# Attention with its softmax sums taken in the first pass over the scores, on one Trainium2 core

## The chip, the core and the metric

The program runs on one core of a Trainium2 chip. Its time is the device time of one execution in microseconds (us), lower is better. The core has five engines that run in parallel, each an in-order queue: TensorE (PE in the profile, with PEld its weight loads), VectorE (DVE), ScalarE (ACT), GpSimd (POOL) and SyncE (SP), which here only issues DMAs. They are kept in step by semaphores. PSUM has eight banks of 128 partitions x 512 fp32 numbers; matmuls write there, ScalarE and VectorE read and write it, GpSimd doesn't.

## What is computed

One block of a diffusion transformer on a batch of 16 sequences of 256 tokens, 512 channels, 16 heads of 32: self-attention, cross-attention to a context of 256 tokens, and a feed-forward layer, each after a modulated layer norm. Cut to what matters:

```python
def _attn(q, k, v):
    scores = jnp.einsum('bqhd,bkhd->bhqk', q, k) / math.sqrt(HEAD_DIM)
    w = jax.nn.softmax(scores, axis=-1)
    return jnp.einsum('bhqk,bkhd->bqhd', w, v).reshape(B, L, D_MODEL)

xn = _adaln(x, noise_emb, ln1_w, ln1_b)          # (x - mu) / std * (1 + gamma) + beta
q, k, v = split(xn @ qkv_w.T)                    # q, k rotated (_rope)
x = x + _attn(_rope(q), _rope(k), v) @ sa_out_w.T
xn = _adaln(x, noise_emb, ln2_w, ln2_b)
x = x + _attn(_rope(xn @ q_w.T), _rope(context @ k_w.T), context @ v_w.T) @ ca_out_w.T
xn = _adaln(x, noise_emb, ln3_w, ln3_b)
x = x + gelu(xn @ ffn_w1.T + ffn_b1) @ ffn_w2.T + ffn_b2
```

## The kernel before

It has two stages. The attention stage, some 1308 us, works off 32 items (16 sequences in each of two layers), and the FFN stage follows. The change touches the attention stage.

Everything is fp32, and products are made of split operands: a number is kept as a high part (rounded to the fast fp32r format) and a low part (the rest), so a projection is three matmuls, hi x hi, hi x lo and lo x hi (L589, L593).

**The order.** `stage_order` writes out one list of steps by hand, and each engine walks that list and picks its own steps. Time is counted in places: three to a head, 48 to an item of 16 heads, 24 to a group G of eight heads (HG = 8), 12 to a half group or quad of four (OH = 4). Part 0 of head n is its scores, part 1 the weigh matmuls of head n - 8 (LAG = 8). In between stand the projections for the items ahead: q at places 52 to 65 (that is 4 to 17 of the next item), v at 66 to 76, the first half of k at 29, the output projection `o` of the item before at 36 to 44, the second half of k at 45.

**A head.** Scores are made twice. The first time (L603, query on the partitions, two matmuls of 256 columns) VectorE takes the row maxima of both halves in one reduction (L851, `neg_max`). For each four heads `max_split` splits the maxima in a high and a low part (L859, L862), `max_turn` transposes them (L612), and `max_copy` has ScalarE copy the eight rows below the queries' 96 rows of `qT`, once for each of the four heads (L729, 8 x 1024). The second time (L623, key on the partitions, 104 rows deep) the maximum is thus taken off inside the matmul, and ScalarE takes the exponential into `prob` (L737).

**The sum.** GpSimd adds the two halves of `prob` (L908). At each `mix`, one for four heads, TensorE multiplies `prob` by the values (L636: 32 columns of the array for each head, four heads side by side, 16 matmul records) into the one bank of `ps_o`, and then multiplies the halves' sums by a matrix of ones (L643, 8 records), which gives the softmax denominators. Then come `invert` (L744 logarithm, L746 exponential of its negative, both ScalarE), `divide` (L867, VectorE), `o_split` (L753, ScalarE) and `o_low` (L896, GpSimd), two places apart.

**Around it.** The modulated norm of x is turned through PSUM in `turn_x` (TensorE L566) and scaled there by ScalarE with gamma and beta from memory (L692). A rotated projection is two VectorE products with cosine and sine (L822, L826), an addition on GpSimd (L902), `rope_high` on ScalarE (L722), `rope_low` on VectorE (L843), a spill to DRAM and later a stacked load into `qT` and `kT` by SyncE.

**Banks.** Four banks of `ps_s` go round among scores, weigh and max_turn (`score_bank`); TensorE waits until the user four turns back has been read (`scores_left`). Three banks `ps_g` serve the projections, one is `ps_o`.

## Time and profile before

| | before |
|---|---|
| times of three runs | 1989.99, 1990.77, 1994.31 us |
| median | 1990.77 us |
| span of the profiled execution | 1991.3 us |
| TensorE busy | 1955.2 us |
| VectorE busy | 1335.1 us |
| ScalarE busy | 1221.5 us |
| GpSimd busy | 1097.4 us |

The profiled execution took 0.5 us more than the median. In the rows below a group of instructions has the form: line, engine, operation, output <- inputs, shapes, count | busy us in all, mean ns of one | idle time of the engine just before them, and what ended it. Busy time counts overlapping instructions once, so busy time over count can be less than the mean of one.

### The profile page before, as it was taken

The numbers are of one execution on the slowest core, as the hardware profiler recorded it, in microseconds if no ns is written. First come the engines' busy times: TensorE is split into PE (matmuls) and PEld (weight loads), VectorE is DVE, ScalarE is ACT, GpSimd is POOL, SyncE is SP. The second block draws the span as 40 slices with busy tenths as digits, with TensorE's granted clock in tenths as the row PEclk, the third lists the DMA queues.
The fourth block names the chain that finished last, engine by engine and source line by source line (L and its number), as shares of the span: only waits on it lengthen the run. The fifth ranks groups of instructions, "written<-read, shape, count | busy, mean of one in ns | idle before, by whom it ended". The sixth has DMA issues, their size and how long they took to land. (4 is left out here: it accounts for less than half of the span.)

```text
span 1991.3 us, 40759 instructions
## 1 busy us (share of the span) xinstructions
PE 1955.2 (98%) x14612; PEld 1666.6 (84%) x14612; DVE 1335.1 (67%) x2317; ACT 1221.5 (61%) x2277; POOL 1097.4 (55%) x1205
## 2 busy tenths in 40 slices
PE   7999999999999999999999999899999999999999
PEld 6788888888887888888888887678998989989998
DVE  6866776776677676666667666545676676666654
ACT  3565566666666666666666666655656666666654
POOL 2555566566666676766666676523444363553531
PEclk9999999999999999999999999999999999999999
DMA  7877667676778686667667676543322323232230
GB/s 245 219 203 182 173 172 193 162 192 177 179 196 224 174 222 192 180 192 207 186 173 206 190 180 177 152 133 97 115 82 78 107 64 96 85 95 88 63 96 32
DMA packets 300197, 307.53 MB, mean 154 GB/s; under 512 B 15840, under 2 KB 253664, under 8 KB 300000
## 3 DMA queue, kind: packets, MB, share of 16 engines
q1 hardware_dynamic: 299408, 304.45, 55.4%
q8 instruction: 121, 1.98, 0.4%
q14 instruction: 76, 0.62, 0.1%
q10 hardware_dynamic: 592, 0.47, 0.1%
HBM read 212.59 MB, written 92.27 MB: 153 GB/s over the span
## 5 line engine op out<-in xcount | busy, mean ns | idle before, releaser
L908 POOL TENSOR_TENSOR sums_sb<-prob 128x256 f32<-128x256 f32 x512 | 405.1, 796 | 323.1 <-ACT prob L737 321.8
L851 DVE TENSOR_REDUCE neg_max<-ps_s 128x2 f32<-128x512 f32 x512 | 347.7, 686 | 335.2 <-PE ps_s L603 332.8
L737 ACT ACTIVATE prob<-ps_s 128x512 f32<-128x512 f32 x512 | 304.6, 596 | 348.6 <-PE ps_s L623 343.3
L902 POOL TENSOR_TENSOR rope_c<-rope_c,rope_s 128x512 f32<-128x512 f32 x128 | 179.0, 1398 | 115.9 <-DVE rope_s L826 115.1
L603 PE MATMUL ps_s<-kT,qT 96*128 96x256 f32 x1024 | 225.0, 301 | 2.3 <-DMA qT<-q_turned 2.3
L603 PEld LDWEIGHTS ps_s<-kT,qT 96*128 96x128 f32 x1024 | 164.5, 190 | 65.5 <-issue 53.9
L623 PE MATMUL ps_s<-qT,kT 104*128 104x256 f32 x1024 | 207.7, 284 | 10.0 <-ACT qT L729 7.2
L593 PE MATMUL ps_g<-xx_hi,w_hi 128*128 128x256 f32 x1024 | 210.4, 287 | 3.4 <-DVE rope_s L826 2.0
L593 PE MATMUL ps_g<-xx_hi,w_lo 128*128 128x256 f32 x1024 | 205.4, 282 | 0.0
L593 PE MATMUL ps_g<-xx_lo,w_hi 128*128 128x256 f32 x1024 | 204.8, 281 | 0.0
L1266 PE MATMUL ps_y<-w_hi,h_hi 128*128 128x512 f32 x512 | 201.5, 393 | 1.2 <-DVE h_lo L1391 1.2
L623 PEld LDWEIGHTS ps_s<-qT,kT 104*128 104x128 f32 x1024 | 170.6, 190 | 36.4 <-ACT qT L729 13.9
L1266 PE MATMUL ps_y<-w_lo,h_hi 128*128 128x512 f32 x512 | 200.6, 392 | 0.0
L1266 PE MATMUL ps_y<-w_hi,h_lo 128*128 128x512 f32 x512 | 199.4, 389 | 0.0
L1391 DVE TENSOR_TENSOR h_lo<-h_sb,h_hi 128x512 fp32r<-128x512 f32 x128 | 111.2, 872 | 103.7 <-ACT h_hi L1289 102.4
L1250 PE MATMUL ps_h<-xf_hi,cw_hi 128*128 128x256 f32 x592 | 167.4, 283 | 0.0
L1250 PE MATMUL ps_h<-xf_lo,cw_hi 128*128 128x256 f32 x592 | 165.8, 280 | 0.0
L1250 PE MATMUL ps_h<-xf_hi,cw_lo 128*128 128x256 f32 x592 | 165.7, 280 | 0.0
L593 PEld LDWEIGHTS ps_g<-xx_hi,w_hi 128*128 128x128 f32 x1024 | 158.4, 190 | 8.5 <-issue 5.2
L593 PEld LDWEIGHTS ps_g<-xx_lo,w_hi 128*128 128x128 f32 x1024 | 158.7, 191 | 0.0
L593 PEld LDWEIGHTS ps_g<-xx_hi,w_lo 128*128 128x128 f32 x1024 | 158.0, 190 | 0.0
L729 ACT ACTIVATE qT<-ps_s 8x1024 fp32r<-8x1024 f32 x128 | 130.4, 1018 | 3.1
(157 smaller groups left out, 4823.7 us busy)
## 6 DMA issues: line engine op xcount, KB each, us to landing
kT<-k_turned SPq DMA_DIRECT2D x192, 256.0 KB, 4.8
qT<-q_turned SPq DMA_DIRECT2D x64, 512.0 KB, 7.0
f_raw<-in_w1T SPq DMA_DIRECT2D x124, 256.0 KB, 3.1
k_turned<-rot_hi SPq DMA_DIRECT2D x64, 256.0 KB, 4.2
k_turned<-rot_lo SPq DMA_DIRECT2D x64, 256.0 KB, 4.3
q_turned<-rot_hi SPq DMA_DIRECT2D x64, 256.0 KB, 2.5
q_turned<-rot_lo SPq DMA_DIRECT2D x64, 256.0 KB, 2.6
qT<-q_turned SPq DMA_DIRECT2D x64, 256.0 KB, 7.5
```

What stands on the lines that cost most here:

```text
L593: ins = eng.matmul(ps_g[:, b, s * L:(s + 1) * L], w[:, row, (T * s + t) * P:(T * s + t + 1) * P], a[:, c, :], start=c == 0 and j == 0 and ...
L603: ins = eng.matmul(ps_s[:, score_bank(step), t * L:(t + 1) * L], qT[0:ROWS, G % NG, j, t * P:(t + 1) * P], kT[0:ROWS, G % NG, j, :], start ...
L623: ins = eng.matmul(ps_s[:, score_bank(step), t * L:(t + 1) * L], kT[:, G % NG, j, t * P:(t + 1) * P], qT[:, G % NG, j, :], start=True, sto ...
L729: eng.activation(qT[ROWS:MROWS, G % NG, OH * half:OH * (half + 1), :], ps_s[ROWS:MROWS, score_bank(step), 0:L].unsqueeze(1).broadcast_to([ ...
L737: eng.activation(prob[:, n % NP, :, :].rearrange("p t l -> p (t l)"), ps_s[:, score_bank(step), :], ACT.Exp, scale=HD ** -0.5).then_inc(ex ...
L851: eng.tensor_reduce(neg_max[G % 2][:, :, j], ps_s[:, score_bank(step), :].rearrange("p (t l) -> p t l", l=L), AX.X, ALU.max, negate=True). ...
L902: eng.tensor_tensor(rope_c[n % 2][:, :, :], rope_c[n % 2][:, :, :], rope_s[:, :, :], ALU.add).then_inc(rope_added, 1)
L908: eng.tensor_tensor(sums_sb[:, n % NP, :], prob[:, n % NP, 0, :], prob[:, n % NP, 1, :], ALU.add).then_inc(halves_added, 1)
L1250: ins = eng.matmul(ps_h[:, bank(p, n), 0:L], w[:, cols], x_[:, k, :], start=n in OPENS and k == 0 and j == 0, stop=k == 1 and j == 2, skip ...
L1266: ins = eng.matmul(ps_y[:, t, :], h[:, t * P:(t + 1) * P], w, start=c == 0 and j == 0, stop=c == FC - 1 and j == 2)
L1391: eng.tensor_tensor(h_lo[a % NH][:, :], h_sb[a % 2][:, :], h_hi[a % NH][:, :].bitcast(F32), ALU.subtract).then_inc(h_lo_done, 1)
```

## The change

The softmax denominators come from the first pass. A new step `total` has ScalarE run over each score bank in place after the maximum: exponential with the negative maximum as bias and an accumulated sum, one instruction for each half (256 columns). For four heads a step `log` takes the logarithm of the sums, and `max_split` takes it off the negative maxima before it splits them. So the second pass gives normalised weights at once: the addition on GpSimd, the ones matmuls, `invert` and `divide` are gone. The scale of the scores moves into cosine and sine on the host.

`mix` now takes eight heads, 32 matmul records, into a bank of `ps_s`, which has five banks and one more kind of user; `prob` holds ten heads. `o_split` and `o_low` work on 512 columns straight from PSUM, `o_low` on VectorE. `max_copy` writes one head's rows (256 columns), and `max_spread` has VectorE copy them to the other three. `turn_x` is scaled by VectorE from item 2 on. `rope_low` moves from VectorE to GpSimd, whose rotary addition becomes a subtraction and an addition of half the width. Some projections stand one place later. Not shown: the narrower sine, buffers that hold the first parameters, the names of semaphores, and the same shifts by one place on other lines.

```diff
+BY_ACT = 2
...
-            late = {N: 24, N + 1: 14}.get(ahead, 0)
+            late = {N: 26, N + 1: 14}.get(ahead, 0)
...
-                turns(shares((p + 29, 6, k[:4]), (p + 45, 7, k[4:])))
+                turns(shares((p + 29, 6, k[:4]), (p + 46, 7, k[4:])))
...
-            spread(p + 36, 9, [("project", "o", i - 1, t, c) for cs in (range(KC - 1), (KC - 1,)) for t in range(T) for c in cs])
-            put(p + 47, "store", i - 1)
+            spread(p + 37, 9, [("project", "o", i - 1, t, c) for cs in (range(KC - 1), (KC - 1,)) for t in range(T) for c in cs])
+            put(p + 48, "store", i - 1)
...
-            put(24 * G + 12 * half + 10, "max_split", G, half)
+            put(24 * G + 12 * half + 12, "log", G, half)
+            put(24 * G + 12 * half + 13, "max_split", G, half)
             put(24 * G + 12 * half + 19, "max_turn", G, half)
             put(24 * G + 12 * half + 20, "max_copy", G, half)
+            put(24 * G + 12 * half + 23, "max_spread", G, half)
...
-    for quad in range(4 * N):
-        place = 3 * (4 * quad + LAG + 5) + 2
-        for n, kind in enumerate(("mix", "invert", "divide", "o_split", "o_low")):
-            put(place + 2 * n, kind, quad)
+    for G in range(2 * N):
+        place = 3 * (8 * G + LAG + 9) + 2
+        for n, kind in enumerate(("mix", "o_split", "o_low")):
+            put(place + n, kind, G)
...
+            if part == 2 and n < HEADS:
+                yield ("total", n)
...
-    score_users = [step for step in order if step[0] in ("scores", "weigh", "max_turn")]
+    score_users = [step for step in order if step[0] in ("scores", "weigh", "max_turn", "mix")]
     score_turn = {step: n for n, step in enumerate(score_users)}
-    NS = 4
+    NS = 5
...
-            NP = 6
+            NP = 10
...
-                return {"scores": max_done, "weigh": exp_done, "max_turn": maxes_copied}[old[0]], nth[old]
+                return {"scores": total_done, "weigh": exp_done, "max_turn": maxes_copied, "mix": o_lo_done}[old[0]], nth[old]
...
-                        if j % OH == 0:
-                            eng.wait_ge(maxes_copied, nth["max_turn", G, j // OH])
+                        if j % OH < 2:
+                            eng.wait_ge(maxes_spread if j % OH else maxes_copied, nth["max_turn", G, j // OH])
...
-                        quad = step[1]
-                        i, c = divmod(quad, KC)
-                        eng.wait_ge(exp_done, OH * (quad + 1))
-                        if c == 0:
+                        G = step[1]
+                        i, g = divmod(G, 2)
+                        b = score_bank(step)
+                        eng.wait_ge(exp_done, HG * (G + 1))
+                        if g == 0:
                             eng.wait_ge(v_done, values[i, 1])
-                        if quad:
-                            eng.wait_ge(o_divided, quad)
-                        for k in range(T):
-                            for j in range(OH):
-                                ins = eng.matmul(ps_o[j * HD:(j + 1) * HD, 0, 0:L],
-                                                 v_sb[i % NV][:, k, c * P + j * HD:c * P + (j + 1) * HD],
-                                                 prob[:, (OH * quad + j) % NP, k, :], start=k == 0, stop=k == T - 1)
-                        if quad == 0:
-                            eng.wait_ge(ones_set, 1)
-                        eng.wait_ge(halves_added, OH * (quad + 1))
-                        for j in range(OH):
-                            ins = eng.matmul(ps_o[j * HD:(j + 1) * HD, 0, L:2 * L], ones[:, :],
-                                             sums_sb[:, (OH * quad + j) % NP, :], start=True, stop=True)
-                        ins.then_inc(mix_done, 1)
+                        for c in (2 * g, 2 * g + 1):
+                            cols = slice((c % 2) * L, (c % 2 + 1) * L)
+                            for k in range(T):
+                                for j in range(OH):
+                                    n = OH * (KC * i + c) + j
+                                    ins = eng.matmul(ps_s[j * HD:(j + 1) * HD, b, cols],
+                                                     v_sb[i % NV][:, k, c * P + j * HD:c * P + (j + 1) * HD],
+                                                     prob[:, n % NP, k, :], start=k == 0, stop=k == T - 1)
+                            ins.then_inc(mix_done, 1)
...
+                        if i >= BY_ACT:
+                            continue
...
-                        eng.activation(qT[ROWS:MROWS, G % NG, OH * half:OH * (half + 1), :],
-                                       ps_s[ROWS:MROWS, score_bank(step), 0:L].unsqueeze(1).broadcast_to([2 * OH, OH, L]),
+                        eng.activation(qT[ROWS:MROWS, G % NG, OH * half, :], ps_s[ROWS:MROWS, score_bank(step), 0:L],
                                        ACT.Copy).then_inc(maxes_copied, 1)
+                    elif kind == "total":
+                        n = step[1]
+                        G, j = divmod(n, HG)
+                        eng.wait_ge(max_done, n + 1)
+                        if j == 0 and G >= 2:
+                            eng.wait_ge(log_done, 2 * (G - 1))
+                        scores = ps_s[:, score_bank(("scores", n)), :]
+                        for t in range(T):
+                            ins = eng.activation(scores[:, t * L:(t + 1) * L], scores[:, t * L:(t + 1) * L], ACT.Exp,
+                                                 bias=neg_max[G % 2][:, t, j:j + 1], accum_out=total[G % 2][:, t, j:j + 1])
+                        ins.then_inc(total_done, 1)
+                    elif kind == "log":
+                        G, half = step[1:]
+                        eng.wait_ge(total_done, HG * G + OH * (half + 1))
+                        if nth[step] > 2:
+                            eng.wait_ge(shift_done, nth[step] - 2)
+                        eng.activation(log_sb[half][:, :, :], total[G % 2][:, :, OH * half:OH * (half + 1)], ACT.Ln).then_inc(log_done, 1)
                     elif kind == "weigh":
                         n = step[1]
                         eng.wait_ge(weigh_done, n + 1)
                         if n >= NP:
                             eng.wait_ge(mix_done, (n - NP) // OH + 1)
-                        eng.activation(prob[:, n % NP, :, :].rearrange("p t l -> p (t l)"), ps_s[:, score_bank(step), :], ACT.Exp,
-                                       scale=HD ** -0.5).then_inc(exp_done, 1)
-                    elif kind == "invert":
-                        quad = step[1]
-                        eng.wait_ge(mix_done, quad + 1)
-                        if quad:
-                            eng.wait_ge(o_lo_done, quad)
-                        eng.activation(o_sb[:, :], ps_o[:, 0, L:2 * L], ACT.Ln).then_inc(log_done, 1)
-                        eng.wait_ge(log_done, quad + 1)
-                        eng.activation(o_sb[:, :], o_sb[:, :], ACT.Exp, scale=-1.0).then_inc(den_inverted, 1)
+                        eng.activation(prob[:, n % NP, :, :].rearrange("p t l -> p (t l)"), ps_s[:, score_bank(step), :],
+                                       ACT.Exp).then_inc(exp_done, 1)
                     elif kind == "o_split":
-                        quad = step[1]
-                        i, c = divmod(quad, KC)
-                        eng.wait_ge(o_divided, quad + 1)
-                        if i and c == 0:
+                        G = step[1]
+                        i, g = divmod(G, 2)
+                        eng.wait_ge(mix_done, 2 * (G + 1))
+                        if i and g == 0:
                             eng.wait_ge(product_done, products["o", i - 1, 1])
-                        eng.activation(o_hi[:, c, :], o_sb[:, :], ACT.Copy).then_inc(o_hi_done, 1)
...
-                    elif kind == "rope_low":
-                        n = ropes[step[1:]]
-                        if n > NT:
-                            eng.wait_ge(*rot_free(n))
-                        eng.wait_ge(rot_hi_done, n)
-                        eng.tensor_tensor(rot_lo[:, n % NT, :, :], rope_c[n % 2][:, :, :],
-                                          rot_hi[:, n % NT, :, :].bitcast(F32), ALU.subtract).then_inc(rot_lo_done, 1)
...
                         eng.wait_ge(max_done, HG * G + OH * (half + 1))
                         if nth[step] > 1:
                             eng.wait_ge(max_turned, nth[step] - 1)
+                        eng.wait_ge(log_done, nth[step])
                         mine = neg_max[G % 2][:, :, OH * half:OH * (half + 1)]
-                        eng.tensor_reduce(max_parts[:, :, ROWS:ROWS + OH].bitcast(F32R), mine.unsqueeze(3), AX.X,
+                        eng.tensor_tensor(shift[:, :, :], mine, log_sb[half][:, :, :], ALU.subtract).then_inc(shift_done, 1)
+                        eng.wait_ge(shift_done, nth[step])
+                        eng.tensor_reduce(max_parts[:, :, ROWS:ROWS + OH].bitcast(F32R), shift[:, :, :].unsqueeze(3), AX.X,
                                           ALU.max).then_inc(max_hi_done, 1)
                         eng.wait_ge(max_hi_done, nth[step])
-                        eng.tensor_tensor(max_parts[:, :, ROWS + OH:MROWS], mine, max_parts[:, :, ROWS:ROWS + OH],
+                        eng.tensor_tensor(max_parts[:, :, ROWS + OH:MROWS], shift[:, :, :], max_parts[:, :, ROWS:ROWS + OH],
                                           ALU.subtract).then_inc(max_split, 1)
-                    elif kind == "divide":
-                        quad = step[1]
-                        eng.wait_ge(den_inverted, quad + 1)
-                        eng.tensor_tensor(o_sb[:, :], ps_o[:, 0, 0:L], o_sb[:, :], ALU.mult).then_inc(o_divided, 1)
+                    elif kind == "o_low":
+                        G = step[1]
+                        eng.wait_ge(o_hi_done, G + 1)
+                        chunks = slice(2 * (G % 2), 2 * (G % 2) + 2)
+                        eng.tensor_tensor(o_lo[:, chunks, :], ps_s[:, score_bank(("mix", G)), :].rearrange("p (c l) -> p c l", l=L),
+                                          o_hi[:, chunks, :].bitcast(F32), ALU.subtract).then_inc(o_lo_done, 1)
+                    elif kind == "turn_x" and step[1] >= BY_ACT:
+                        i, half = step[1:]
+                        layer, b = divmod(i, B)
+                        if half == 0:
+                            eng.wait_ge(mod_added, nth["mod_add", layer, 1])
+                            if i < B or i >= N_ITEMS:
+                                eng.wait_ge(x_low_done, nth["x_low", i - 1, 1])
+                            else:
+                                eng.wait_ge(ctx_low_done, 2 * (i - B + 1))
+                        eng.wait_ge(x_turned, nth[step])
+                        for c in range(2):
+                            k = 2 * half + c
+                            ins = eng.tensor_scalar(xT[:, k, :], ps_g[:, bank(step), c * L:(c + 1) * L],
+                                                    gb[:, layer, k, b:b + 1], gb[:, layer, KC + k, b:b + 1], ALU.mult, ALU.add)
+                        ins.then_inc(x_full, 1)
+                    elif kind == "max_spread":
+                        G, half = step[1:]
+                        eng.wait_ge(maxes_copied, nth[step])
+                        rows = qT[ROWS:MROWS, G % NG, OH * half:OH * (half + 1), :]
+                        eng.tensor_copy(rows[:, 1:OH, :], rows[:, 0:1, :].broadcast_to([2 * OH, OH - 1, L])).then_inc(maxes_spread, 1)
...
-                    elif kind == "o_low":
-                        quad = step[1]
...
-                        eng.tensor_tensor(rope_c[n % 2][:, :, :], rope_c[n % 2][:, :, :], rope_s[:, :, :], ALU.add).then_inc(rope_added, 1)
-                    elif kind == "weigh":
-                        n = step[1]
-                        eng.wait_ge(exp_done, n + 1)
-                        if n >= NP:
-                            eng.wait_ge(mix_done, (n - NP) // OH + 1)
-                        eng.tensor_tensor(sums_sb[:, n % NP, :], prob[:, n % NP, 0, :], prob[:, n % NP, 1, :],
-                                          ALU.add).then_inc(halves_added, 1)
+                        eng.tensor_tensor(rope_c[n % 2][:, 0, :], rope_c[n % 2][:, 0, :], rope_s[:, 0, :], ALU.subtract)
+                        eng.tensor_tensor(rope_c[n % 2][:, 1, :], rope_c[n % 2][:, 1, :], rope_s[:, 1, :], ALU.add).then_inc(rope_added, 1)
+                    elif kind == "rope_low":
...
```

## Rows read from the trace of the kernel before

**Rows 1.** Busy us of each engine, share of the span, instructions; from the page.

```profile
PE 1955.2 (98%) x14612; PEld 1666.6 (84%) x14612; DVE 1335.1 (67%) x2317; ACT 1221.5 (61%) x2277; POOL 1097.4 (55%) x1205
```

**Rows 2.** Stretches: length; busy us (instructions) of PE, PEld, DVE, ACT, POOL; clock, DMA, GB/s.

```profile
100.00:1250.00 1150.00, 1140.66 (x9409) 952.33 (x9407) 798.13 (x1459) 729.49 (x1344) 741.03 (x824) 1.00 0.71 188
295.39:305.88 10.49, 10.49 (x78) 8.48 (x77) 6.03 (x12) 8.58 (x17) 7.04 (x8) 1.00 0.60 201
305.88:315.98 10.10, 10.10 (x79) 8.27 (x78) 6.63 (x11) 5.45 (x10) 6.88 (x10) 1.00 0.83 178
315.98:325.43 9.45, 9.45 (x85) 8.24 (x84) 7.20 (x17) 4.52 (x8) 4.61 (x7) 1.00 0.53 159
325.43:333.91 8.48, 8.48 (x83) 7.56 (x82) 7.17 (x13) 5.45 (x10) 5.20 (x6) 1.00 0.73 173
```

**Rows 3.** Timeline of TensorE around one mix: start, us, line, operation.

```profile
498.18 0.40 PE L593 MATMUL ps_g<-xx_lo,w_hi 128*128 128x256 f32 x2
498.51 1.07 PE L636 MATMUL ps_o<-prob,v_sb 128*32 128x256 f32 x16
499.40 0.61 PE L643 MATMUL ps_o<-sums_sb,ones 128*32 128x256 f32 x8
499.94 0.50 PE L603 MATMUL ps_s<-kT,qT 96*128 96x256 f32 x2
```

**Rows 4.** Slices of that mix: L636's matmuls alone on TensorE.

```profile
498.58:498.64 0.06, 0.06 (x4) 1.00 0.56 119
498.88:498.94 0.06, 0.06 (x8) 1.00 1.09 375
```

**Rows 5.** Groups of TensorE's instructions, whole span.

```profile
L643 PE MATMUL ps_o<-sums_sb,ones 128*32 128x256 f32 x1024 | 79.3, 381 | 0.9 <-POOL sums_sb L908 0.9
L603 PE MATMUL ps_s<-kT,qT 96*128 96x256 f32 x1024 | 225.0, 301 | 2.3 <-DMA qT<-q_turned 2.3
```

**Rows 6.** Groups of ScalarE's instructions, whole span.

```profile
L737 ACT ACTIVATE prob<-ps_s 128x512 f32<-128x512 f32 x512 | 304.6, 596 | 348.6 <-PE ps_s L623 343.3
L729 ACT ACTIVATE qT<-ps_s 8x1024 fp32r<-8x1024 f32 x128 | 130.4, 1018 | 3.1
L692 ACT ACTIVATE xT<-ps_g,gb 128x256 f32<-128x256 f32 x136 | 69.1, 560 | 24.4 <-PE ps_g L566 23.9 <-DVE gb L797 0.5
L746 ACT ACTIVATE o_sb<-o_sb 128x256 f32<-128x256 f32 x128 | 53.6, 418 | 4.0
L744 ACT ACTIVATE o_sb<-ps_o 128x256 f32<-128x256 f32 x128 | 48.6, 379 | 1.3 <-PE ps_o L643 1.3
L1371 ACT ACTIVATE h_sb<-ps_h,b_sb 128x256 f32<-128x256 f32 x56 | 26.4, 472 | 61.5 <-PE ps_h L1250 61.5
```

**Rows 7.** Timeline of ScalarE, two neighbours that don't depend on each other.

```profile
303.44 0.60 ACT L737 ACTIVATE prob<-ps_s 128x512 f32<-128x512 f32 x1
303.93 0.59 ACT L715 ACTIVATE v_sb<-ps_g 128x512 f32<-128x512 f32 x1
```

**Rows 8.** Groups of VectorE's instructions; L862 by its least, median and longest ns.

```profile
L843 DVE TENSOR_TENSOR rot_lo<-rope_c,rot_hi 128x512 fp32r<-128x512 f32 x128 | 106.2, 830 | 17.4 <-ACT rot_hi L722 17.4
L867 DVE TENSOR_TENSOR o_sb<-ps_o,o_sb 128x256 f32<-128x256 f32 x128 | 53.2, 416 | 8.9 <-ACT o_sb L746 8.8
...
L862 DVE TENSOR_TENSOR max_parts<-neg_max,max_parts x128: 166/482/1182, 56.0 to 1289.4; 128x8 f32<-128x8 f32 x128
```

**Rows 9.** Groups of GpSimd's instructions, whole span.

```profile
L908 POOL TENSOR_TENSOR sums_sb<-prob 128x256 f32<-128x256 f32 x512 | 405.1, 796 | 323.1 <-ACT prob L737 321.8
L902 POOL TENSOR_TENSOR rope_c<-rope_c,rope_s 128x512 f32<-128x512 f32 x128 | 179.0, 1398 | 115.9 <-DVE rope_s L826 115.1 <-issue 0.3
```

**Rows 10.** Waits of TensorE's weight loads: us in all, times, longest.

```profile
PEld ps_s L623 <- ACT qT L729: 13.9, 21, 2.3
```

**Rows 11.** Stretches near the end of the attention stage.

```profile
1218.87:1287.82 68.95, 63.53 (x535) 50.82 (x534) 49.31 (x95) 47.35 (x89) 42.40 (x50) 1.00 0.66 161
1232.93:1239.96 7.03, 6.13 (x63) 5.07 (x62) 6.90 (x12) 4.92 (x10) 6.36 (x8) 1.00 0.33 110
```

67 lines of the change are left out of this document (33 added, 34 removed).

## The prediction

> **What bounds the kernel now.** I read the page's busy shares first: TensorE is busy for 98% of the span, the next engine for 67% [rows 1]. The table of stretches then says how full the other engines are in the attention stage: between 100 and 1250 us TensorE is busy 1140.66 of 1150 us, VectorE 798.13, ScalarE 729.49, GpSimd 741.03, at a granted clock of 1.00 [rows 2]. So TensorE sets the time, and only 9.3 us of that stretch are its idle time. The kernel repeats itself with a period of one batch item, 38.5 us. I cut one item at the four first mix matmuls of its mixes and get quarters of 10.49, 10.10, 9.45 and 8.48 us, with ScalarE busy for 8.58, 5.45, 4.52 and 5.45 of them [rows 2]; counted back from the hand-written order, these are places 17-29, 29-41, 41-53 and 5-17 of an item's 48. The FFN stage behind attention isn't touched. The chain of the page ends in that stage and so says nothing on the change; I don't use it.
>
> **What leaves TensorE.** Ahead of a mix the last two projection matmuls start at 498.18 and, one step of 0.12 later, 498.30; the 16 mix matmuls start at 498.51, the 8 ones matmuls at 499.40, the next scores at 499.94 [rows 3]. A matmul of this shape lasts 0.38 us (the group of the ones matmuls, [rows 5]), and slices of 60 ns show 4 of them running at first and 8 later [rows 4]: four column groups start together, a new round before the last has ended. 16 matmuls in 1.07 us make four rounds: (1.07 - 0.38) / 3 = 0.23, and 0.89 / 4 = 0.222 us a round. The whole place from 498.30 to 499.94 is 1.64 us, of which 0.12 is the normal step, so a mix of four heads costs 1.52 us: 0.21 to the first round, five steps of 0.222, 0.32 from the last round to the next work, less 0.12. The new mix of eight heads has eight rounds and one entry and exit: 0.21 + 7 x 0.222 + 0.32 - 0.12 = 1.96 us, in place of 2 x 1.52 = 3.04. Saved: 1.08 us for each of 64 groups of eight heads, **69 us**. By item, TensorE falls from 38.5 to 36.3 us. The ones matmuls' own group is busy 79.3 us [rows 5], but that counts the last one's full 0.38 us, which overlaps its neighbours. Mix matmuls, scores, weigh and projections keep their counts.
>
> **What ScalarE gets.** Per item it is now busy 729.49 / 1150 x 38.5 = 24.4 us [rows 2]. Leaving: the logarithm 4 x 0.38, its exponential 4 x 0.42, the copy of maxima 4 x 1.02, o_split 4 x 0.42 (a copy of the exponential's size), and turn_x 69.1 / 34 = 2.03 [rows 6]. Coming: copies of 256 columns on 8 partitions, priced as the 128x256 row at 4 x 0.38; o_split in halves, 2 x 0.60; the new logarithm of 8 numbers per partition, between its fixed part, 0.16 (0.379 - 256 x (0.596 - 0.379) / 256 = 0.16), and 0.38, taken as 0.30, 4 times. That leaves 17.35 us an item before the new sums. These are 32 half-score exponentials per item, 128x256, PSUM to PSUM, with a bias from memory and an accumulated sum. The nearest row is GELU from PSUM with a bias, 472 ns against 379 without [rows 6], and ScalarE starts an independent instruction 0.11 us before the last ends (303.44 + 0.60 against 303.93) [rows 7], so 0.38 us in pace. No row shows an accumulated sum. Bounds: 0 and the fixed part of one more instruction, 0.16, with the overlap lost (0.63 in all). I take 0.10 more, 0.48 us: nearer to the plain row, since it is the same engine pass. 32 x 0.48 = 15.4, ScalarE 32.7 of 36.3 us an item, **90%**; at 0.38 it is 29.5 us (81%), at 0.63 it is 37.5 us (103%).
> The Trainium skill, "ScalarE: Activation LUTs", sections "Step-by-step: what each stage is for" and "What ACT_TABLE_LOAD costs", says that each pointer operand adds about 93 ns, that neighbours overlap by as much, and that writing PSUM is quicker than SBUF; the first two agree with [rows 6, 7], and no run here shows the third yet. By its formula a half would take about an estimated 0.40 us in pace, without the sum; the accumulated sum has no price there.
>
> **Where ScalarE binds inside an item.** The quarters don't share evenly, and the mixes now sit at places 5 and 29 only. TensorE: 10.49 - 1.52 = 9.0; 10.10 - 1.52 + 1.96 = 10.5; 9.45 - 1.52 = 7.9; 8.48 - 1.52 + 1.96 = 8.9. ScalarE, quarter by quarter: old time, less 1.86 for logarithm, exponential, o_split and the smaller copy, less 2.03 of turn_x in the first, plus 0.3 for the log, 0.6 for o_split in the second and fourth, plus 8 x 0.48: 8.8, 8.3, 6.8, 8.3. So in the first quarter the two engines are nearly even, in the other three TensorE is clearly the longer. What decouples them: five score banks shared by everything, so that weigh matmul k + 5 turns needs the total of a score made 7 places earlier, and the weigh at place 25 needs the maxima copied at place 20, 5 places or 3.8 us ahead. TensorE waited for that copy before too: 13.9 us, 21 times, up to 2.3, with ScalarE at 63% [rows 10]. With ScalarE at 90% I add half a microsecond an item, **+15 us** over 30 items (bounds: 0, since no quarter is longer on ScalarE, and 1.6 us an item, rival B).
>
> **VectorE and GpSimd.** VectorE loses rot_lo (4 x 0.83 an item) and the division (4 x 0.42), and gets turn_x (4 x 0.42, priced as the division row, one 256-column pass from PSUM), o_low (2 x 0.7, between the division's 0.42 and rot_lo's 0.83 at twice the division's columns), the spread (4 x 0.6, from the same two rows) and the shift [rows 8]. The shift is one more 8-element subtraction; the one that exists takes 166, 482 or 1182 ns (min, median, max) [rows 8], so 4 x 0.5. From 26.7 to 29.2 us an item, 80% of 36.3: hidden behind TensorE, and if that cover went it would cost its 2.5 us. GpSimd loses 16 x 0.79 and gains rot_lo at about 1.3 a piece against 1.40 for its 512-column addition [rows 9], some 15 of 36.3 us: hidden. What is queued behind the new waits: max_split on VectorE now waits for the log on ScalarE; behind it stand the next score maxima and the rotary products, which free the projection banks. SyncE's spills stand 0.5 us longer for rot_lo, and with them the stacks, the x loads and the stores queued behind; TensorE waited 2.3 us in all for stacks before [rows 5], so 0.5 us stays covered.
> The Trainium skill, "SBUF — State Buffer", in its terms (shared port pair), speaks against the shift: a VectorE instruction with two SBUF inputs and a GpSimd one that reads SBUF exclude each other. The 166 to 1182 ns agree, and by that rule each shift may wait out a GpSimd instruction; with the sums gone it would meet fewer.
>
> **Ends.** From 1218.87 to 1287.82 us few projections are left: TensorE is busy 63.53 of 68.95 us, ScalarE 47.35 [rows 11]. For eight quarters ScalarE gets 8 x (3.84 - 1.26) = 20.6 more, less 2.0 of turn_x: 66 us, against 68.95 less 8 x 0.54 = 64.6 for the stretch if TensorE set it. The light quarter of 7.03 us (ScalarE 4.92) [rows 11] goes to 7.5, not to 6.5. Taking the longer engine in each of the eight gives about no gain there: **+4 us** on the sum. The start has a chain of rotations through GpSimd, with 1.3 in place of 0.83 us for rot_lo and some queueing: **+1**. The last mix is followed by two steps, not four, but leaves two chunks of the output projection behind it: 0. Edits with one answer: sine and cosine scaled on the host, the narrower sine, parameter loads all into prob, places moved by one: 0.
>
> **Sum.** The profiled execution spans 1991.3 us, 0.5 above the median of the three, 1990.77. 1991.3 - 69 + 4 + 1 + 15 = 1942.3, less 0.5 = **1942 us** rounded.
>
> **Rivals.**
> A. ScalarE binds: the accumulated sum is an instruction of its own without overlap. For: no row prices it. At 0.63 us a half 37.5 us an item, 1.2 above TensorE, 30 x 1.2 = 36, with 14 for ends (10) and start (4), estimates scaled up from the 4 and 1 above: 1991 - 69 + 14 + 36 = 1972. It begins at (36.3 - 17.35) / 32 = 0.59 us a half. Against: that lies 0.11 us above the price taken, more than a second memory operand costs (0.09).
> B. The new chain (total, log, shift, split, turn, copy, spread) locks the engines: VectorE stands at max_split while ScalarE is behind, ScalarE then lacks the next maximum. Against: ten places, 7.5 us, from scores at 9 to max_turn at 19, hold a 512-column VectorE pass (0.83 at most, [rows 8]), 0.96, 0.3 and three small passes, 2.6 to 4.6 us. If each of four times an item costs 0.4 us, 1.6 x 32 = 51 in place of 15: 1978.
> C. Slower: the exponential that reads and writes one PSUM bank runs at half rate: 0.48 + 256 x 0.85 / 1000 = 0.70 us. ScalarE 17.35 + 22.4 = 39.7 an item against the old 38.5: 32 x 1.2 + 5 + 6: 2040. It decides from (38.5 - 17.35) / 32 = 0.66 us a half. Against: this kernel has no such instruction to judge by, but reading PSUM alone is no slower than SBUF (379 against 418 ns, [rows 6]). The Trainium skill, "PSUM — Partial Sum Buffer", section "Specifications (TRN2)", names full bandwidth unless two engines meet in one bank, and here only one is in the bank.
> D. It doesn't do what it says: the ones rounds were filling time that TensorE would spend waiting anyway. The 100% busy quarters say no [rows 2]; it would be 1991.
>
> **Chances.** Forecast, with 1916 to 1958 of its own: 0.65. A or B, 1958 to 1986: 0.21. D or a half-way mix within 0.2% (1987 to 1995; 0.2% is about what a measurement of this kernel can tell from no change): 0.05. C and other slower outcomes: 0.09. Range 1916 to 1985: its low end is the whole 69 with most of the 9.3 us of TensorE's idle time gone too as the copy gets shorter, its high end A or B with some more of the ends' cost. Faster 0.86, same 0.05, slower 0.09.
>
> **What would show it.** Right: TensorE's attention stage shorter by 50 or so, no ones row, one 32-matmul mix of about 1.9 us; total rows at 0.45 to 0.5 us; ScalarE near 90%; VectorE near 80%. Wrong: total rows above 0.59 us, or TensorE idle for more than 1 us an item at weigh or scores, released by ScalarE; or a period of the steady items that isn't near 36.8 us.

## The result and the profile after

| | before | after |
|---|---|---|
| median | 1991.30 us (4 runs) | 1967.95 us (4 runs, 1963.51 to 1972.09) |
| span of the profiled execution | 1991.3 us | 1961.7 us |

The ratio is 0.9878, with a 95% interval of 0.986 to 0.9896: faster by 1.2%, 23 us, where the prediction said 2.5%, 49 us. The time lies in the range and near none of the rivals but A (1972), whose mechanism turns out to be the wrong one. The profiled execution was the fastest of the four, 4.4 us under their median; sums below are made on the spans: 1991.3 - 1961.7 = 29.6 us gained.

The page of the changed kernel, busy us of each engine, to be held against [rows 1], and two rows of its slices of the span:

```profile
PE 1902.3 (97%) x13588; PEld 1653.0 (84%) x13588; DVE 1418.4 (72%) x2509; ACT 1458.3 (74%) x4005; POOL 783.0 (40%) x820
...
PE   7899999999999999999999998899999999999999
...
PEclk9899999999999999999999999999999999999999
```

TensorE did 1024 fewer matmuls and was busy 52.9 us less, not 69. Its idle time went from 1991.3 - 1955.2 = 36.1 to 59.4 us. Both halves of the shortfall stand there already: 23.3 us more of standing still, and 16.2 us more of busy time than the count of matmuls explains. The attention stage in one row, and the two halves of an item in each layer, cut at its mixes (columns as in [rows 2]):

```profile
100.00:1250.00 1150.00, 1120.23 (x8729) 962.26 (x8729) 906.51 (x1699) 984.14 (x3050) 459.45 (x478) 0.99 0.75 194
346.40:364.28 17.88, 17.88 (x141) 15.36 (x140) 13.27 (x28) 15.15 (x50) 3.43 (x4) 1.00 0.82 217
364.28:383.63 19.35, 18.98 (x149) 16.16 (x149) 15.58 (x29) 16.28 (x50) 10.73 (x11) 1.00 0.64 150
842.08:860.15 18.07, 17.79 (x121) 14.48 (x120) 14.28 (x29) 15.02 (x49) 5.59 (x6) 1.00 0.92 268
860.15:878.78 18.63, 18.63 (x170) 17.30 (x169) 15.53 (x28) 17.24 (x53) 10.88 (x12) 1.00 0.60 136
```

An item lasts 37.2 us in layer 0 and 36.7 in layer 1, where 36.3 was forecast without stalls. ScalarE is busy for 31.4 of 37.2 us (84%) and VectorE for 28.9 (77%). TensorE's idle time in the long stretch is 29.8 us, 9.3 before [rows 2].

The parts of the change, as the trace has them. First TensorE's timeline around a mix (start, us, line, operation), then groups of the whole span on ScalarE, VectorE and GpSimd:

```profile
346.07 0.40 PE L597 MATMUL ps_g<-xx_lo,w_hi 128*128 128x256 f32 x2
346.40 1.93 PE L642 MATMUL ps_s<-prob,v_kept 128*32 128x256 f32 x32
348.27 0.50 PE L607 MATMUL ps_s<-kT,qT 96*128 96x256 f32 x2
```

```profile
L738 ACT ACTIVATE ps_s<-ps_s,neg_max 128x256 f32<-128x256 f32 x1024 | 459.3, 451 | 85.1 <-DVE neg_max L853 81.6
L738 ACT ACTIVATION_READ_ACCUMULATOR ps_s<-ps_s,neg_max 128x1 f32 x1024 | 213.7, 209 | 0.0
L728 ACT ACTIVATE qT<-ps_s 8x256 fp32r<-8x256 f32 x128 | 48.3, 378 | 3.1
L746 ACT ACTIVATE log_sb<-total 128x8 f32<-128x8 f32 x128 | 26.7, 209 | 3.8
...
L894 DVE CAST qT<-qT 8x768 fp32r<-8x768 f32 x128 | 121.4, 949 | 9.8 <-ACT qT L728 6.3
L887 DVE TENSOR_SCALAR xT<-ps_g,gb 128x256 f32<-128x256 f32 x128 | 63.3, 537 | 0.0
L862 DVE TENSOR_TENSOR shift<-neg_max,log_sb 128x8 f32<-128x8 f32 x128 | 48.2, 376 | 38.7 <-ACT log_sb L746 36.8
L873 DVE TENSOR_TENSOR o_lo<-ps_s,o_hi 128x512 fp32r<-128x512 f32 x64 | 43.7, 683 | 12.7 <-ACT o_hi L760 12.7
...
L930 POOL TENSOR_TENSOR rot_lo<-rope_c,rot_hi 128x512 fp32r<-128x512 f32 x128 | 165.8, 1300 | 50.2 <-ACT rot_hi L721 49.1
```

From the last projection pair at 346.07 to the mix are 0.33 us and from there to the scores 1.87; less two normal steps of 0.12 that is 1.96 us, the mix of the sum. Two halves of one total on ScalarE:

```profile
350.26 0.45 ACT L738 ACTIVATE ps_s<-ps_s,neg_max 128x256 f32<-128x256 f32 x1
350.62 0.20 ACT L738 ACTIVATION_READ_ACCUMULATOR ps_s<-ps_s,neg_max 128x1 f32 x1
350.71 0.45 ACT L738 ACTIVATE ps_s<-ps_s,neg_max 128x256 f32<-128x256 f32 x1
```

And who kept TensorE's weight loads waiting (us, times, longest), to be held against [rows 10]:

```profile
PEld ps_s L607 <- ACT ps_s L738: 19.4, 34, 1.8
PEld ps_s L627 <- ACT ps_s L738: 13.1, 17, 1.7
```

The wait for the copied maxima is gone as a large one, and the total, which now keeps a score bank, has taken its place.

**Where the gain went.** The mix of group G stands at the same place as the second mix of its pair did before, so their starts cut both traces at the same points. "Due" is the length before less 1.08 us for each of the groups in it (for the first stretch less one mix of four, 1.52; for the last plus 0.44, the longer mix):

| stretch, by the start of a mix | before | due | after | lost | of it idle |
|---|---|---|---|---|---|
| start to G 0 | 87.20 | 85.68 | 97.26 | 11.6 | 6.6 |
| G 0 to 8 | 161.18 | 152.54 | 155.32 | 2.8 | 0.9 |
| G 8 to 24, layer 0 | 308.20 | 290.92 | 297.86 | 6.9 | 3.1 |
| G 24 to 34, change of layers | 202.74 | 191.94 | 199.77 | 7.8 | 5.3 |
| G 34 to 56, layer 1 | 427.06 | 403.30 | 403.05 | -0.3 | 2.7 |
| G 56 to 63, end | 115.59 | 108.03 | 117.05 | 9.0 | 3.3 |
| G 63 to the end of the program | 689.33 | 689.77 | 691.39 | 1.6 | 1.4 |

That is 39.5 us lost out of 69.1. 28.4 of them lie in three short stretches, at the start, at the change of layers and at the end, which together make a fifth of the program; the long stretch of layer 1 came out at what was due. Idle is not all of it. TensorE's own rows, columns: length, busy (instructions), granted clock, DMA share, GB/s:

```profile
50.00:55.00 5.00, 3.62 (x22) 0.61 1.10 343
55.00:60.00 5.00, 5.00 (x33) 0.71 1.11 218
85.00:90.00 5.00, 3.03 (x11) 0.52 0.83 268
90.00:95.00 5.00, 5.00 (x25) 0.50 0.74 182
615.00:620.00 5.00, 2.13 (x13) 0.77 0.97 238
620.00:625.00 5.00, 5.00 (x18) 0.55 1.11 278
1165.00:1170.00 5.00, 1.95 (x9) 0.73 0.53 115
1170.00:1175.00 5.00, 4.98 (x41) 0.59 0.95 320
```

Between 90 and 95 us TensorE worked without a gap at 1.2 GHz. Taken over all the 5 us stretches, TensorE had some 37 us of time at 1.2 GHz, all in these three parts of the program, against 3 before. These are six episodes of 3.4 to 10.2 us, each beside a stop of TensorE of 1.2 to 3.4 us: behind it, or begun in its last microsecond. Not every such stop has one: behind those of 1.4 to 1.9 us that end at 66, 76, 606, 721 and 1195 us the clock stayed at 1.00 in this execution. The busy time above the due one in the same three parts is 5.0, 2.6 and 5.7 us. (Not all of such an excess is the clock: G 8 to 24 has one of 3.8 us at a clock of 1.00. A matmul's span of 0.40 overlaps the next, 0.24 later, so a stop shorter than the overlap counts as busy.) The traces of the experiments, which follow, go the same way. In the end stretch, G 56 to 63, TensorE does the same 782 matmuls in e10, e9, after and e12; it was busy there for 99.1, 100.4, 103.1 and 104.5 us, at a mean granted clock of 0.99, 0.96, 0.94 and 0.93.

### The profile page after: what moved, and what is told of

Same layout as the page of the kernel before. It is cut to its first block and busy times, and to the rows that moved or that the text cites. A ratio compares the mean times of both kernels' runs of the same rounds, so it can differ in the third digit from the quotient of the medians.

```text
span 1961.7 us, 39861 instructions
## 1 busy us (share of the span) xinstructions
PE 1902.3 (97%) x13588; PEld 1653.0 (84%) x13588; DVE 1418.4 (72%) x2509; ACT 1458.3 (74%) x4005; POOL 783.0 (40%) x820
## 5 line engine op out<-in xcount | busy, mean ns | idle before, releaser
L738 ACT ACTIVATE ps_s<-ps_s,neg_max 128x256 f32<-128x256 f32 x1024 | 459.3, 451 | 85.1 <-DVE neg_max L853 81.6
L853 DVE TENSOR_REDUCE neg_max<-ps_s 128x2 f32<-128x512 f32 x512 | 352.7, 690 | 162.7 <-PE ps_s L607 158.8
L923 POOL TENSOR_TENSOR rope_c<-rope_c,rope_s 128x256 f32<-128x256 f32 x128 | 98.6, 770 | 425.2 <-DVE rope_s L834 425.2
L627 PE MATMUL ps_s<-qT,kT 104*128 104x256 f32 x1024 | 213.8, 291 | 21.0 <-ACT ps_s L738 6.4
L607 PE MATMUL ps_s<-kT,qT 96*128 96x256 f32 x1024 | 218.0, 295 | 10.7 <-DMA qT<-q_turned 5.4
L607 PEld LDWEIGHTS ps_s<-kT,qT 96*128 96x128 f32 x1024 | 172.3, 193 | 54.8 <-ACT ps_s L738 19.4
L738 ACT ACTIVATION_READ_ACCUMULATOR ps_s<-ps_s,neg_max 128x1 f32 x1024 | 213.7, 209 | 0.0
L627 PEld LDWEIGHTS ps_s<-qT,kT 104*128 104x128 f32 x1024 | 168.8, 193 | 50.6 <-issue 19.4
L930 POOL TENSOR_TENSOR rot_lo<-rope_c,rot_hi 128x512 fp32r<-128x512 f32 x128 | 165.8, 1300 | 50.2 <-ACT rot_hi L721 49.1
```

Of the source, the lines that this page charges most:

```text
L607: ins = eng.matmul(ps_s[:, score_bank(step), t * L:(t + 1) * L], qT[0:ROWS, G % NG, j, t * P:(t + 1) * P], kT[0:ROWS, G % NG, j, :], start ...
L627: ins = eng.matmul(ps_s[:, score_bank(step), t * L:(t + 1) * L], kT[:, G % NG, j, t * P:(t + 1) * P], qT[:, G % NG, j, :], start=True, sto ...
L738: ins = eng.activation(scores[:, t * L:(t + 1) * L], scores[:, t * L:(t + 1) * L], ACT.Exp, bias=neg_max[G % 2][:, t, j:j + 1], accum_out= ...
L853: eng.tensor_reduce(neg_max[G % 2][:, :, j], ps_s[:, score_bank(step), :].rearrange("p (t l) -> p t l", l=L), AX.X, ALU.max, negate=True). ...
L923: eng.tensor_tensor(rope_c[n % 2][:, 0, :], rope_c[n % 2][:, 0, :], rope_s[:, 0, :], ALU.subtract)
L930: eng.tensor_tensor(rot_lo[:, n % NT, :, :], rope_c[n % 2][:, :, :], rot_hi[:, n % NT, :, :].bitcast(F32), ALU.subtract).then_inc(rot_lo_d ...
```

## The experiments

Each was timed in three rounds beside the kernel before; times are medians. "After" is the changed kernel, 1968 us. The lengths are those of the stretches of the table above, from each profiled execution; since after's lies 4.4 us under its median, a gain on after looks smaller by about that much in the stretches than in the medians, and a loss larger:

| kernel | us | ratio, 95% interval | to G 0 | 0-8 | 8-24 | 24-34 | 34-56 | 56-63 |
|---|---|---|---|---|---|---|---|---|
| after | 1967.95 | 0.986-0.9896 | 97.3 | 155.3 | 297.9 | 199.8 | 403.1 | 117.1 |
| e1 ones off | 1939.12 | 0.9726-0.9758 | 86.1 | 154.2 | 294.3 | 193.6 | 408.0 | 109.8 |
| e2 first 8 low parts | 1958.98 | 0.9826-0.9855 | 92.1 | 155.3 | 297.7 | 199.8 | 403.6 | 118.0 |
| e3 no read | 1956.07 | 0.9803-0.9833 | 98.3 | 153.7 | 294.5 | 197.2 | 401.2 | 118.4 |
| e4 filling | 1970.01 | 0.9877-0.9906 | 100.2 | 158.6 | 297.7 | 201.3 | 403.1 | 117.1 |
| e5 four banks | 2007.87 | 1.0065-1.0095 | 98.7 | 160.5 | 308.1 | 207.3 | 417.2 | 121.7 |
| e6 x by ScalarE | 1980.22 | 0.9925-0.9955 | 96.8 | 156.9 | 300.9 | 201.1 | 409.8 | 119.5 |
| e7 whole copy | 1986.26 | 0.9957-0.9978 | 97.4 | 157.9 | 305.7 | 202.3 | 409.8 | 120.3 |
| e8 rounds back | 2017.91 | 1.0115-1.0145 | 100.2 | 162.3 | 311.5 | 205.2 | 422.1 | 123.8 |
| e9 no total | 1941.47 | 0.9732-0.9766 | 96.0 | 153.0 | 293.1 | 193.5 | 399.3 | 114.0 |
| e10 total aside | 1954.30 | 0.9796-0.9826 | 97.5 | 153.0 | 293.1 | 200.1 | 403.6 | 114.3 |
| e11 all low parts | 1960.84 | 0.9828-0.9857 | 88.9 | 156.3 | 299.8 | 202.1 | 403.8 | 117.2 |
| e12 total first | 1956.20 | 0.9798-0.9831 | 88.8 | 154.7 | 296.5 | 201.5 | 405.0 | 118.6 |

**Is the work that left worth its time?** e1 takes the ones matmuls and their additions out of the kernel before and changes nothing else. It leaves out the softmax denominators; the logarithm becomes a copy of the same size, so that ScalarE keeps its work.

```diff
-                        for j in range(OH):
-                            ins = eng.matmul(ps_o[j * HD:(j + 1) * HD, 0, L:2 * L], ones[:, :],
-                                             sums_sb[:, (OH * quad + j) % NP, :], start=True, stop=True)
...
-                    elif kind == "weigh":
...
-                        eng.activation(o_sb[:, :], ps_o[:, 0, L:2 * L], ACT.Ln).then_inc(log_done, 1)
+                        eng.activation(o_sb[:, :], ps_o[:, 0, 0:L], ACT.Copy, scale=0.0).then_inc(log_done, 1)
```

> The kernel before without the ones matmuls (8 records at each of 128 mixes) and without GpSimd's additions of the halves; the logarithm is replaced by a copy with scale 0 of the same size, so the values aren't divided. It measures the first term of my sum alone: two rounds of 0.222 us at each mix, 128 x 0.444 = 57 us, with the four-head mixes kept. If the term is right: 1934 us, ratio 0.971. If the ones rounds filled time that TensorE would have lost anyway (rival D): above 1970 us.

It gave 52.5 us. 128 x 2 x 0.222 = 57 was the term, and the rounds are paid in every stretch: 109.8 us at the end is 5.8 shorter than before, with 6.2 due. Rival D falls. The reverse, on the changed kernel: e8 multiplies the first product of each chunk twice (four rounds more for each group).

```diff
                             cols = slice((c % 2) * L, (c % 2 + 1) * L)
+                            for j in range(OH):
+                                eng.matmul(ps_s[j * HD:(j + 1) * HD, b, cols],
+                                           v_sb[i % NV][:, 0, c * P + j * HD:c * P + (j + 1) * HD],
+                                           prob[:, (OH * (KC * i + c) + j) % NP, 0, :], start=True, stop=True)
                             for k in range(T):
```

> The changed kernel with the first product of each chunk made twice, that is the two rounds that the ones matmuls took, four per group of eight heads: TensorE gets 64 x 0.89 = 57 us of work back, nothing else changes. If TensorE binds throughout: +57 us against the changed kernel, 2025. If part of its time is standing still in which the extra work hides: 30 to 50 us, 1998 to 2018; the steady layer-1 items +1.78 us each, and the layer-0 items and the end less.

50 us of 57 came back: 13.7 of 14.2 in the stretch 8-24, 19.0 of 19.6 in 34-56, 6.7 of 6.2 at the end, but only 5.4 of 8.9 at the change of layers. So TensorE's work still sets the pace nearly everywhere, and what the change lost it lost beside that work, not by TensorE having slack.

**The start.** In the changed kernel a rotation's low part stands in GpSimd's queue, and SyncE's spill waits for it. The timeline of after, GpSimd and SyncE before the first scores (start, us, line, operation, idle time ahead and its releaser):

```profile
38.36 1.18 POOL L924 TENSOR_TENSOR rope_c<-rope_c,rope_s 128x256 f32<-128x256 f32 x1
39.50 3.44 POOL L930 TENSOR_TENSOR rot_lo<-rope_c,rot_hi 128x512 fp32r<-128x512 f32 x2
39.57 0.63 ACT L721 ACTIVATE rot_hi<-rope_c 128x512 fp32r<-128x512 f32 x1 [3.31 <-POOL rope_c L924]
41.26 0.55 SPq L987 DMA_DIRECT2D k_turned<-rot_lo  x1
41.85 0.62 SPq L998 DMA_DIRECT2D qT<-q_turned  x1
...
49.55 0.47 PE L607 MATMUL ps_s<-kT,qT 96*128 96x256 f32 x2 [3.40 <-DMA qT<-q_turned]
```

and the same of before:

```profile
36.42 0.68 DVE L843 TENSOR_TENSOR rot_lo<-rope_c,rot_hi 128x512 fp32r<-128x512 f32 x1
36.65 1.60 POOL L902 TENSOR_TENSOR rope_c<-rope_c,rope_s 128x512 f32<-128x512 f32 x1 [0.40 <-DVE rope_s L826]
37.13 0.55 SPq L965 DMA_DIRECT2D k_turned<-rot_lo  x1
37.73 0.66 SPq L976 DMA_DIRECT2D qT<-q_turned  x1
...
46.49 0.47 PE L603 MATMUL ps_s<-kT,qT 96*128 96x256 f32 x2 [0.96 <-DMA qT<-q_turned]
```

GpSimd takes 1.7 us for a low part there (3.44 for two), VectorE took 0.68; the load of q's stack is issued 4.1 us later, the first scores start 3.1 later, TensorE stands for 3.4 us, and behind that its clock is at 0.61 and 0.71. e2 gives the low parts of the first 8 rotations back to VectorE, with a semaphore of their own; e11 gives it all 128; e4 leaves them and puts 12 small matmuls of no use ahead of each wait for a stack or for maxima in the first 16 heads, so that TensorE doesn't stand still. Of e2's edit the line that takes the later rotations for GpSimd is shown; the same subtraction stands on VectorE for the first 8:

```diff
-                    elif kind == "rope_low":
+                    elif kind == "rope_low" and ropes[step[1:]] > FIRST:
```

> The changed kernel with the low part of the first 8 rotations (items 0 and 1) back on VectorE. Theory S (the start lost 10 us because these subtractions queue on GpSimd, the first scores came 3 us later, TensorE idled and its granted clock fell to 1.2 GHz in two stretches before 100 us): first scores near 46.5 us, the mix of the first eight heads at 87 to 91 us instead of 97.3, the total 6 to 10 us below the changed kernel (1958 to 1962). Rival (the start is late because of the fuller ScalarE and the longer way to the second weigh matmul): no more than 2 us gained.

> The changed kernel with every low part of the rotations on VectorE, as before the change, not only those of the first 8. Theory of the start: the gain of the first 8 (9 us) is all there is, and in the steady items VectorE goes from about 79% to 88% busy (4 x 0.8 us an item), which costs a little: 1958 to 1970 us. Rival: the low parts on GpSimd delay the spills and stacks in every item and at the change of layers, and this kernel is faster than 1955 us.

```diff
+            def fill(eng, step, count):
+                for _ in range(count):
+                    eng.matmul(ps_s[0:ROWS, score_bank(step), 0:ROWS], ident[:, 0:ROWS], ident[:, 0:ROWS], start=True, stop=True)
...
+                        if j == 0 and n < 16:
+                            fill(eng, step, 12)
```

> The changed kernel with 12 small matmuls (96x96, of no use, into the bank that the step overwrites) ahead of each wait of the first 16 heads for stacks or maxima. They take about 12 x 0.12 to 0.3 us each time, seven times or so, in time that TensorE mostly waits. If the clock falls because TensorE stands still there and the fall costs time: granted clock 1.00 up to 100 us and the time 2 to 6 us below the changed kernel. If the waits set the time and the clock costs nothing: same time or up to 5 us longer.

e2's median is 9 us under after's; in the traces 5.1 us are gone up to G 0 (8.4 in e11's) and the middle is unchanged. The first scores start at 48.4 us in e2's trace, at 46.4 in e11's and 46.5 before. e12, below, has the start of e2 and reads 46.5 and 88.8, so e2's own trace shows the low end of the gain. e11 gets nothing more: what it wins at the start it gives back in layer 0 and at the change of layers, with VectorE 45 us busier. So the low parts on GpSimd cost 5 to 9 of the 11.6 us at the start, and nothing in the steady items. e4 did what it should to the clock between 50 and 60 and between 85 and 95 us, and got nothing for it. Its first mix came 3.0 us later than after's, but that isn't the dummies' doing alone: in e8, with nothing added ahead of it, it came as late (100.2 us), and first scores start at 50.5 to 51.9 us in every trace that leaves all low parts on GpSimd, only in after's at 49.6. The stretch 0-8 is 3.3 us longer, with dummies in its first places. So e4 doesn't settle what the slow clock costs by itself; there is only the account of busy time above.

**The banks, or ScalarE's load?** After [rows 10]'s wait vanished, 32.5 us of waits are ended by the total. It can keep TensorE waiting in two ways: because ScalarE has too much to do, or because a bank is held through a maximum and two exponentials. e3 drops the accumulator's read (the softmax denominators are left out, the logarithm is a copy), which takes 96 us of work off ScalarE; e5 takes one of five score banks away; e6 has ScalarE scale all of x; e7 has ScalarE copy the maxima to all four heads as before (8 x 1024), with no spread.

```diff
-                                                 bias=neg_max[G % 2][:, t, j:j + 1], accum_out=total[G % 2][:, t, j:j + 1])
+                                                 bias=neg_max[G % 2][:, t, j:j + 1])
```

> The changed kernel without the accumulated sum (no accumulator read, 1024 of them, 0.09 us each in pace); the logarithm is a copy with scale 0, so the weights aren't normalised. ScalarE gets 92 us of room over the attention stage. Rival A in its mild form (ScalarE's fullness costs TensorE its gain everywhere): 15 to 25 us below the changed kernel, the layer-1 items shorter than 36.6 us. Theory (TensorE binds in the items of layer 1, ScalarE only at the ends and in some of the items of layer 0): layer-1 items stay at 36.6 us, the stretch from 1153 us on and the layer-0 items gain, 8 to 15 us in all.

```diff
-    NS = 5
+    NS = 4
```

> The changed kernel with four score banks in place of five (the fifth is left empty). In the changed kernel a score bank is held through the maximum and two exponentials on ScalarE (0.7 + 0.9 us and the queues), not only the maximum. Bank theory (the light stretches at the end of attention are set by how long banks are held): the last 15 groups' stretch, 117 us, grows by 8 us or more, and TensorE's waits for total and exponential rows grow; the steady items of layer 1 grow too, by over 0.5 us each; 1985 us or more. ScalarE theory (its fullness sets them): banks don't matter, below 1975 us.

```diff
-BY_ACT = 2
+BY_ACT = 99
```

> The changed kernel with the modulation of x back on ScalarE for all items, 2 us an item more there (31.4 to 33.4 of 37.2 us in layer 0), 2 less on VectorE. If ScalarE's fullness costs time: 0.5 to 1 us an item, 15 to 30 us slower than the changed kernel, 1980 to 1995. If TensorE binds in steady items: within 5 us of it.

```diff
-                        eng.activation(qT[ROWS:MROWS, G % NG, OH * half, :], ps_s[ROWS:MROWS, score_bank(step), 0:L],
+                        eng.activation(qT[ROWS:MROWS, G % NG, OH * half:OH * (half + 1), :],
+                                       ps_s[ROWS:MROWS, score_bank(step), 0:L].unsqueeze(1).broadcast_to([2 * OH, OH, L]),
```

> The changed kernel with the maxima copied for four heads at once on ScalarE (1.02 us in place of 0.38) and no spread on VectorE (0.95 us). One link less between transposed maxima and the second weigh matmul, 2.6 us an item more on ScalarE, 3.8 less on VectorE. If ScalarE's fullness decides: 15 to 30 us slower. If the length of the chain through both engines decides (start and end): 0 to 8 us faster.

96 us less work on ScalarE gave 12 us (e3), none of it at the end, where the stretch was even 1.3 longer; 50 us more cost 12 (e6), 72 more cost 18 (e7), though both took 65 and 129 us off VectorE. So ScalarE's load matters, at 0.12 to 0.25 us for each of its own. One bank fewer cost 40 us (e5), in every stretch, most in the steady items (14.1 in 34-56); the end grew by 4.6, where the bank theory had asked for 8 or more. In e5's trace the waits ended by a total grow from 19.4 and 13.1 to:

```profile
PEld ps_s L627 <- ACT ps_s L738: 39.4, 56, 1.9
PEld ps_s L607 <- ACT ps_s L738: 33.4, 80, 1.8
```

e3, e6 and e7 change both things at once, and e5 shows that banks are short, not what holds them. e9 and e10 part the two. e9 has no first-pass exponentials at all: the bank is free after VectorE's maximum. e10 keeps ScalarE's instructions at their places in its queue but lets them read a table and write a buffer of their own, so the bank is free just as early. One more thing differs: e10's `log` still waits for the totals, as after's does, while e9's waits only for the maxima, so e9 also shortens the chain from the scores to the copied maxima. Both leave out the softmax denominators, and e10 uses the sine's table as the cosine's to make room.

The first pair of lines is in both, the second in e10:

```diff
-                return {"scores": total_done, "weigh": exp_done, "max_turn": maxes_copied, "mix": o_lo_done}[old[0]], nth[old]
+                return {"scores": max_done, "weigh": exp_done, "max_turn": maxes_copied, "mix": o_lo_done}[old[0]], nth[old]
...
-                            ins = eng.activation(scores[:, t * L:(t + 1) * L], scores[:, t * L:(t + 1) * L], ACT.Exp,
+                            ins = eng.activation(aside[:, t, :], cos_sb[:, :], ACT.Exp,
```

> The changed kernel without the first-pass exponentials: the score bank is free after VectorE's maximum, and the logarithm's step copies zeros, so the weights are not normalised (the softmax denominators are left out). Against the changed kernel (1968 us) this takes away both what the total does to ScalarE (about 0.92 us a head) and what it does to the banks. TensorE's instructions are the same, so the steady items can give back only TensorE's idle time. Expected by both theories: 1935 to 1950 us, and the end stretch from the mix of group 56 to that of group 63 goes from 117.05 to 108 to 111 us. If the end stretch stays above 114 us, neither the banks nor ScalarE set it and the new mix, the turned maxima or VectorE do.

> The changed kernel with the first-pass exponentials at the same places of ScalarE's queue, but read from a table in SBUF and written to a buffer of their own (16-bit output), so that ScalarE has the same work (a little more, if reading SBUF is dearer) while the score bank is free as soon as VectorE has its maximum. The softmax denominators are left out, and the cosine table is replaced by the sine's to make room, with the same instructions. Theory 1, banks held too long: most of what the kernel without totals gains is gained here too, the end stretch (mix of group 56 to 63) is 108 to 112 us and the time is within 8 us of that kernel's. Theory 2, ScalarE's fullness itself: the end stretch stays at 115 to 119 us and the time at 1955 to 1970 us.

Neither theory has it alone, and the table says where each holds. From G 0 to 24 the two kernels run alike, 153.0 and 293.1 us, 2.3 and 4.7 less than after: there it was the banks, for 7.0 of the 9.7 us lost, and ScalarE's load cost nothing. At the end they are alike too, 114.0 and 114.3, so some 2.9 of the 9.0 lost there are the banks'. At the change of layers it is the other way round: 193.5 without the exponentials, 200.1 with them aside, 199.8 in after. e10's exponential reads SBUF and lasts 500 ns, not 451, so its ScalarE is busier than after's; its 6.6 us are an upper bound for the load's part. Layer 1 goes the same way, 399.3 without and 403.6 aside, 403.1 in after. There TensorE has a single kind of wait, in after and, as 3.9 us, in e10, and none in e9:

```profile
PE ps_s L627 <- ACT qT L728: 3.1, 11, 0.3
```

That is the copy of the maxima, at the end of the chain total, log, split, turn. Whether it comes late because ScalarE is full or because the chain is longer, no run tells: e9 takes both away, e10 keeps both.

In all, the totals cost 26.5 us (e9 against after; 21.4 on the spans), of which 13.7 (8.7) were gone once they had left the banks (e10). Of the 13 that remain, 11 lie at the change of layers and in layer 1 (6.7 and 4.3 between the two traces), and they belong to ScalarE's load and the longer chain together.

**What is left at the end and at the change of layers.** With no totals the end still takes 114.0 us where 108.0 is due and e1 took 109.8. Its idle time before a score or weigh has other releasers there, in e9 (us, times, longest, from 1134.95 to 1248.99):

```profile
PE ps_s L627 <- DVE qT L883: 4.6, 5, 2.4
PE ps_s L607 <- DMA qT<-q_turned: 2.8, 1, 2.8
PE ps_s L627 <- DVE o_lo L862: 2.2, 3, 1.5
```

The first is the spread of the maxima, the third the low part of the mix's output, which holds a score bank. The same bank stands at the longest wait of layer 0's end in after, on VectorE and TensorE:

```profile
614.54 0.69 DVE L853 TENSOR_REDUCE neg_max<-ps_s 128x2 f32<-128x512 f32 x1 [0.65 <-PE ps_s L607]
615.15 1.80 DVE L811 TENSOR_TENSOR w_lo<-w_raw,w_hi 128x512 fp32r<-128x512 f32 x1
616.87 0.98 DVE L887 TENSOR_SCALAR xT<-ps_g,gb 128x256 f32<-128x256 f32 x2
617.78 0.68 DVE L873 TENSOR_TENSOR o_lo<-ps_s,o_hi 128x512 fp32r<-128x512 f32 x1
...
618.51 0.80 PE L627 MATMUL ps_s<-qT,kT 104*128 104x256 f32 x2 [2.87 <-DVE o_lo L873]
```

The mix had ended by 614.0 and ScalarE had read it by 614.8, but `o_low` is queued on VectorE behind a weight's low part and the scaling of x, which came over from ScalarE. TensorE stood for 2.87 us and went on at 1.2 GHz (the rows at 615 and 620 above). No run takes these out one by one, so that they are what remains at the two places is read from the trace, not shown by an experiment.

**A faster version.** e12 is e2, with ScalarE's total of a head ahead of the second exponential of that turn.

```diff
+            if part == 1 and n < HEADS:
+                yield ("total", n)
             if part == 1 and n >= LAG and n - LAG < HEADS:
                 yield ("weigh", n - LAG)
-            if part == 2 and n < HEADS:
-                yield ("total", n)
```

> The kernel with the low parts of the first 8 rotations on VectorE (1959 us), and ScalarE takes the total of a head ahead of the second exponential of that turn, not behind it. ScalarE's work is the same. In the trace of the changed kernel the total of a score whose maximum was taken at 351.62 started only at 352.38, behind the exponential of 351.88; now the score's bank comes free about 0.6 us earlier and the weigh's bank 0.9 us later. Theory of the held banks: it matters only if the score's bank is the one that TensorE asks for next, which the waits say (19 us of TensorE's idle time ended by a total, under 3 by the second exponential): 1950 to 1958 us. Rival: the bank held longer turns into the one waited for, or ScalarE now stands for the maximum while an exponential is ready behind it: 1959 to 1975 us.

At 1956.2 us it is the fastest that computes all of the block, 12 us under after and 35 under before. Its interval (0.9798 to 0.9831) overlaps e2's (0.9826 to 0.9855) by a hair, so the order's own gain of some 3 us is likely and not certain; in the trace the weight loads' waits ended by a total fall to 16.7 us from e2's 18.5 at the scores and to 5.6 from 16.3 at weigh, and the wins of layer 0 (1.2 us in 8-24) are partly given back later.

## Why the prediction was off, point by point

The 69 us were there to be had; what failed is what the sum took off them, 20 us, where 39.5 were lost. Three of its terms were too small: the start, 1 us for 11.6; the ends, 4 for 10.6; and the change of layers, which had no term, 7.8. The first and the last of these were read from durations and shares of steady items; the ends were read from their own rows, but engine by engine, with nothing for banks and latencies. The term for the steady items, 15 for 9.4, was too large and hid 5.6 us of that.

- **What leaves TensorE**: right in each number. Mix 1.96 us, rounds worth 52 of 57 us taken out and 50 of 57 put in; the whole 69 is there as "due", and layer 1 pays all of it.
- **What ScalarE gets**: right. The half exponential runs at a pace of 0.45 us (350.26 to 350.71 above), taken as 0.48. The accumulated sum is a second instruction of 209 ns, but it overlaps its neighbours, and dropping it saved (1458.3 - 1362.0) / 1024 = 0.094 us a half, the 0.10 of the sum. The log was 0.21, not 0.30. ScalarE came to 84%, not 90%. Rival A was wrong in its mechanism: no half is near 0.59 us. The Trainium skill, "ScalarE: Activation LUTs", section "Step-by-step: what each stage is for", says that writing PSUM is quicker than writing SBUF: 451 ns for L738 against 472 for the one row that has a bias and writes SBUF [rows 6], of another function, agree. By the formula of its section "What ACT_TABLE_LOAD costs" the pace without the sum was an estimated 0.40 us; in e3 the two halves of a score start 0.36 us apart, so the measured one is 0.04 less.
- **Where ScalarE binds inside an item**, +15: the size was about right for the steady parts and the reason half right. Lost there were 2.8 + 6.9 - 0.3 = 9.4 us, in layer 0 alone. The prediction put it on ScalarE's load; e9 and e10 show that in layer 0 it was, for 7.0 of the 9.7 us, the time for which a bank is held, which the sum named ("five score banks shared by everything") but never priced: maximum 0.69, a queue, and 0.9 for the two halves, where a maximum alone was before.
- **The start**, +1: this is the step that failed worst, 11.6 us, of which e2, e11 and e12 give 5.1 to 8.5 back. The chain was named, and only the difference of two steady durations (1.3 less 0.83) was charged once; the later spills were put at nothing ("so 0.5 us stays covered"). Three things were missed: in that stretch GpSimd took 1.7 us a low part and 1.2 for a half addition, both of which stand in one queue; the load of the stack is queued on SyncE behind the spill, so the delay reaches TensorE (4.1 us at the load's issue, 3.1 at the first scores); and TensorE then ran on at 1.2 GHz.
- **The change of layers**: not in the sum at all, 7.8 us. The prediction read steady items and the end, and took "80% of 36.3: hidden behind TensorE" as true for every place. There weights are split beside everything else: TensorE's longest wait in that stretch, 2.87 us, was for an `o_low` queued on VectorE behind one. With no totals at all (e9) 1.5 of the 7.8 stay. What each of these steps costs there was not taken apart by a run.
- **Ends**, +4: 10.6 us (9.0 and 1.6). The approach, the longer of two engines in each quarter, has no term for banks or for latencies in a stretch where little other work stands between a score and its weigh. e3 shows that ScalarE's load isn't what sets it.
- **VectorE and GpSimd**: the spread was priced at 0.6 and took 0.949 us; shift 0.376 and `o_lo` 0.683 lay near their 0.5 and 0.7, GpSimd's 1.30 was right. VectorE came to 77%, not 80%. The Trainium skill, "SBUF — State Buffer", section "Who interferes with whom", spoke against the shift as an instruction that may wait out one of GpSimd; its least and longest were 150 and 1135 ns with a median of 168. 29 of the 128 shifts lasted over 300 ns, 1.09 us on average, and each of these ended within 0.25 us behind a GpSimd instruction that was running when it began, so the trace agrees; in the kernel before it was 77 of 128 for the like subtraction (L862 there), so it became rarer, as forecast.
- **Rival B** (the chain total, log, shift, split, turn, copy, spread locks the engines) at 1.6 us an item isn't seen: layer 1's 11 items, at 17.6 us by it, ended 0.3 under what was due. But the chain isn't free there: TensorE's 3.1 us of waits for the copied maxima are its, and without totals (e9) the stretch was 3.7 us shorter. Its last link, the spread, is among the waits of the end.
- **Rival C** falls: 451 ns in place.
- **A price that had no term**: a stall costs TensorE more than its length where the granted clock falls beside it. In the three stretches where it fell, 13.3 us of the 28.4 lost are busy time, next to 15.2 of idle. 34 us more at half the speed is 17 by arithmetic, near the 13.3. The sum could have had it: before had one such fall, at a gap of the same kind:

```profile
1200.00:1205.00 5.00, 3.52 (x31) 0.85 0.88 298
1205.00:1210.00 5.00, 5.00 (x42) 0.81 1.07 219
```

Lost were 39.5 us on the spans where 20 were forecast; with the 4.4 us between after's profiled run and its median and the 1.8 between that run's span and time, this makes the 26 us between 1942 and 1968.

## What to carry to other kernels

Work taken off the bound engine pays best where the pace is steady (10.3 of 17.3 us in the stretch 8-24, all of 23.8 in 34-56); most of the loss comes at the start, at a change of stage and at the end, so read those stretches one by one, with each moved step's place in its new engine's queue and the durations that hold there, not those of the steady state. When a pass is added that reads a buffer in place, price how long it holds the buffer beside how long it keeps its engine; an experiment that runs the pass elsewhere with the same instructions tells the two apart. An engine that was never idle before and now stands for 2 or 3 us may pay for the stop twice (here some did and some didn't).

## What the hardware showed that was not expected

- An activation with an accumulated sum leaves two records, the pass (451 ns) and a read of the accumulator (209 ns), and the read costs 0.094 us in pace.
- A VectorE subtraction of 8 columns with both inputs in SBUF took 150 to 170 ns as a rule and 1.09 us in 29 of 128 cases, each time behind a running GpSimd instruction.
- TensorE's granted clock went to 1.2 GHz beside single stops of 1.2 to 3.4 us, for 3.4 to 10.2 us each time, but not beside every stop of that size, while the same kernel's steady items stayed at 1.00.
- A copy of 8 partitions x 768 from SBUF to SBUF took VectorE 949 ns (948 to 951 in all 128), ScalarE's copy of 8 x 256 from PSUM 378.
- A GpSimd subtraction of 128 x 512 took 1.30 us in the steady state and 1.7 us among the weight splits of the start.
